# One decoder layer on one core: two loop steps swapped, two loads moved into the loop, and the cross attention's row in another order

## What is computed

```python
x = x + attn(layernorm(x))          # gated delta rule with spikes, 8 heads, 64 keys, 128 values
x = x + xattn(layernorm(x), ctx)    # 16 heads of 64, context of 77 tokens
x = x + sign_ffn(layernorm(x))      # 128 -> 512 -> 512 -> 128, weights +1 or -1
```

```python
mem = 0.9 * mem + sd;  hard = mem > 0.5;  mem = mem - 0.5 * spike
s = s * alpha[..., None]
s = s + beta * outer(k, v - k @ s)
out = s @ q
```

## Time and profile before

| | us |
|---|---|
| median of 3 runs | 1318.04 |
| lowest, highest | 1312.53, 1323.74 |
| the profiled execution | 1319.52 |
| its span | 1317.8 |
| PE busy in the span | 1088.8 |
| DVE, ACT, POOL busy | 723.7, 503.0, 203.8 |

### The profile page before, as it was taken

How to read it: one execution, slowest core, us unless ns; L and a number is a source line. 1 busy time by engine, 2 the same in 40 slices (tenths; PEclk the granted TensorE clock), 3 DMA queues, 4 the chain that set the end, 5 groups by cost and what they waited for, 6 DMA issues and landing times. The chain is left out here.

```text
span 1317.8 us, 40766 instructions
## 1 busy us (share of the span) xinstructions
PE 1088.8 (83%) x17172; PEld 792.1 (60%) x17172; DVE 723.7 (55%) x2523; ACT 503.0 (38%) x1445; POOL 203.8 (15%) x381
## 2 busy tenths in 40 slices
PE   1577357999999999999999995777889889898867
PEld 1222126888888888888888883455447445545642
DVE  5657787787788878788665531252226134323500
ACT  1564111244444444444444333243244234424411
POOL 4000210112222112222211201111002001100200
PEclk9688655799999999999998887896989899999969
DMA  2000000000000000000000004000000000000000
GB/s 80 0 1 1 0 0 1 4 4 4 4 4 4 4 3 4 4 4 4 4 4 4 3 3 132 8 0 1 0 8 8 2 9 0 8 0 1 9 0 8
DMA packets 11219, 11.35 MB, mean 9 GB/s; under 512 B 1515, under 2 KB 9311, under 8 KB 11039
## 3 DMA queue, kind: packets, MB, share of 16 engines
q1 hardware_dynamic: 11039, 8.75, 2.2%
HBM read 7.70 MB, written 1.05 MB: 7 GB/s over the span
## 5 line engine op out<-in xcount | busy, mean ns | idle before, releaser
L830 PE MATMUL banks<-work 64*64 64x64 f32 x3072 | 110.0, 236 | 9.6 <-DVE gates L712 6.3
L1006 ACT COPY work<-banks 128x128 f32<-128x128 f32 x160 | 42.9, 268 | 180.9 <-PE banks L860 180.9
L860 PE MATMUL banks<-work,gates 64*64 64x32 f32 x2560 | 109.7, 224 | 1.2 <-issue 1.1
L717 DVE TENSOR_TENSOR work<-work,banks 128x128 f32<-128x128 f32 x128 | 37.0, 289 | 131.5 <-PE banks L870 130.5
L298 DVE SCALAR_TENSOR_TENSOR gates<-mom,gates 128x16 f32<-128x16 f32 x512 | 100.5, 196 | 10.5 <-ACT gates L414 5.9
L880 PE MATMUL banks<-work 64*64 64x32 f32 x2560 | 106.2, 223 | 0.0
L870 PEld LDWEIGHTS banks<-work 64*64 64x64 f32 x2048 | 77.2, 141 | 46.9 <-ACT work L1006 23.5
L870 PE MATMUL banks<-work 64*64 64x32 f32 x2048 | 87.1, 226 | 19.6 <-DVE work L722 16.9
L860 PEld LDWEIGHTS banks<-work,gates 64*64 64x64 f32 x2560 | 95.5, 141 | 12.0 <-issue 11.4
L712 DVE COPY_PREDICATED gates<-work,banks 128x256 f32<-128x256 uint32 x192 | 101.3, 528 | 1.1
L302 DVE SCALAR_TENSOR_TENSOR mom<-gates 128x16 f32<-128x16 f32 x512 | 98.0, 191 | 5.9
(11 more groups left out here) (225 smaller groups left out, 2380.2 us busy)
## 6 DMA issues: line engine op xcount, KB each, us to landing
work<-in_x_dram SPq DMA_DIRECT2D x4, 256.0 KB, 4.3
out_dram<-work SPq DMA_DIRECT2D x4, 256.0 KB, 3.5
gates<-in_w_ff_dram SPq DMA_DIRECT2D x3, 256.0 KB, 4.6
wv_sb<-in_wv_dram SPq DMA_DIRECT2D x1, 512.0 KB, 4.7
work<-in_w_out_dram SPq DMA_DIRECT2D x1, 512.0 KB, 4.9
gates<-in_x_Wq_dram SPq DMA_DIRECT2D x1, 512.0 KB, 6.3
gates<-in_x_Wk_dram SPq DMA_DIRECT2D x1, 512.0 KB, 6.9
gates<-in_x_Wv_dram SPq DMA_DIRECT2D x1, 512.0 KB, 7.8
```

The lines of the kernel that those rows point to most:

```text
L830: last = pe.matmul(level_out(l)[to, a], KS[rows, n.two, hp], late[rows, hp], start=True, stop=True)
L860: last = pe.matmul(packed(psZX, l)[rows, hp], EA[rows, n.three, l, hp], first_half(X, l)[rows, hp], start=True, stop=True)
L1006: ac.copy(first_half(Z[:, l - 1], l), packed(psZX, l)).then_inc(z_ok, 1)
```

## The change

In the loop, add_xt and make_xt go ahead of the level steps. SP loads the context and w_out as soon as the last beta product is done (before, the region that they go to holds gate weights); VectorE scales w_out at the end of its body of round 30. In the tail:

- `front_u1` of rows 1 to 3 goes behind `project_out`; `front_out` is dealt out as (0), (1), (2, 3), (4, 5), (6), (7) instead of (0), (1, 2), (3, 4), (5), (6), (7). The context's transposes go behind `front_u1` of row 0.
- The first output of `connect_second` is made in pieces around `spread_root` and `feed_forward`; `keys` waits for it at its fifth product only.
- `context_values` goes ahead of `spread_root(b, 1)` and uses banks 2 and 7; `queries` uses banks 4 to 6; ScalarE keeps the values ahead of the queries; the scores no longer wait for the values, the first `weigh` does.
- ScalarE keeps a block's weighed sums behind the first kept quarter of the next block; of the last block VectorE keeps one half.

```diff
@@ loop, sync
+                sp.wait_ge(beta_mm, GATES)
+                sp.dma_start(ctx_sb, ctx_in.rearrange("b s d -> s b d")).then_inc(ctx_ld, 16)
+                sp.dma_start(wout_sb, w_out.rearrange("(h v) d -> v h d", v=DV)).then_inc(wout_ld, 16)
@@ loop, vector
+                def scale_out():
+                    ve.wait_ge(wout_ld, 16)
+                    for h in range(2 * HP):
+                        ve.tensor_scalar(wout_sb[:, h, :], wout_sb[:, h, :], v("w_hn", h), None, ALU.mult)\
+                            .then_inc(wout_ok, 1)
...
                         spike(scan, h + 1)
+                        if nxt:
+                            add_xt(nxt, l)
+                        spike(scan, h + 2)
                         if aft:
                             prefix(aft, l)
-                        spike(scan, h + 2)
+                        spike(scan, h + 3)
                         if aft:
                             suffix(aft, l)
-                        spike(scan, h + 3)
+                        spike(scan, h + 4)
                         if aft:
                             keep(aft, l)
-                        spike(scan, h + 4)
-                        if nxt:
-                            add_xt(nxt, l)
...
+                    if cur and cur.it == ROUNDS - 2:
+                        scale_out()
@@ loop, tensor
                             make_x(nxt, l)
+                        if nxt:
+                            make_xt(nxt, l)
                         if aft:
                             level(aft, l)
-                        if nxt:
-                            make_xt(nxt, l)
@@ tail, tensor
-                def connect_second(b, f, ps):
+                def connect_second(b, f, ps, parts):
                     pe.wait_ge(h1_ok, (b + 1) * F2)
                     if f >= 1:
                         pe.wait_ge(h2_ok, b * F2 + f)
-                    for a in range(F2):
+                    for a in parts:
...
-                        if a >= 4:
-                            pe.wait_ge(q2_ok, b * XP + a - 3)
-                        pe.matmul(bank[4 + a % 4][:, :], Wq_sb[:, a, :], n1, start=True, stop=True).then_inc(q2_mm, 1)
+                        if a >= 3:
+                            pe.wait_ge(q2_ok, b * XP + a - 2)
+                        pe.matmul(bank[4 + a % 3][:, :], Wq_sb[:, a, :], n1, start=True, stop=True).then_inc(q2_mm, 1)
...
                 def project_out(b):
-                    pe.wait_ge(xo_done, (b + 1) * 2 * NTB)
+                    pe.wait_ge(xo_done, (b + 1) * (2 * NTB - 1))
+                    pe.wait_ge(xo_late, b + 1)
...
                     if now:
-                        front_u1(b)
+                        if b == 0:
+                            front_u1(b)
+                            turn_context()
+                            pe.wait_ge(wout_ok, 2 * HP)
                         front_out(b, (0,))
                     if b:
                         project_out(done)
+                        if now:
+                            front_u1(b)
...
                     if b:
-                        connect_second(done, 0, bank[1])
+                        connect_second(done, 0, bank[1], (0, 1))
                     if now:
                         spread_root(b, 0)
+                    if b:
+                        connect_second(done, 0, bank[1], (2,))
+                    if now:
                         feed_forward(b)
+                    if b:
+                        connect_second(done, 0, bank[1], (3,))
+                    if now:
...
                         mean_square(b, 1)
+                        context_values(b)
                         spread_root(b, 1)
                         queries(b)
-                        context_values(b)
                         pe.wait_ge(kb_ok, b * 4 + 4)
-                        pe.wait_ge(vb_ok, b * 2 + 2)
@@ tail, scalar
                 def keep_weighed(b, n):
                     ac.wait_ge(weigh_mm, b * NTB + n + 1)
-                    for j in range(2):
+                    for j in range(2 if n + 1 < NTB else 1):
...
                         keep_centred(b, 1)
                         keep_keys(b)
-                        ac.copy(cb, ctxT[:, b]).then_inc(cb_ok, 1)
+                        keep_values(b)
                         for a in range(XP):
...
                             keep_turned(b, n, 0)
+                            if n:
+                                keep_weighed(b, n - 1)
                             keep_turned(b, n, 2)
...
-                        if now:
-                            keep_weighed(b, n)
+                    if now:
+                        keep_weighed(b, NTB - 1)
@@ tail, vector
+                def keep_weighed_late(b):
+                    ve.wait_ge(weigh_mm, (b + 1) * NTB)
+                    for a in range(4):
+                        last = ve.tensor_scalar(XO[:, 4 + a, (NTB - 1) * P:], bank[7][:, a * P:(a + 1) * P],
+                                                v("bv", 4 + a), None, ALU.add)
+                    last.then_inc(xo_late, 1)
...
                 for b in range(B + 1):
                     done, now = b - 1, b < B
+                    if b:
+                        add_attention(done)
                     if now:
                         front_act(b)
...
+                        keep_weighed_late(b)
```

More of the change, by code:

```diff
@@ L457, in _ @@
                             .then_inc(mconst, 1)
+        used[0] = 0
+        wout_sb = region([2 * HP, D])
+        ctx_sb = region([B, D])[0:S]
+        rows_start = used[0]
+        assert rows_start <= HP * P + HP * 2 * DK + HP * P
+        ctx_ld, wout_ld, wout_ok = sem("ctx_ld"), sem("wout_ld"), sem("wout_ok")
         used[0] = kept_end
@@ L597, in decoder_kernel, with _ @@
         with nc.Block() as block:
+            @block.sync
+            def _(sp):
+                sp.wait_ge(beta_mm, GATES)
+                sp.dma_start(ctx_sb, ctx_in.rearrange("b s d -> s b d")).then_inc(ctx_ld, 16)
+                sp.dma_start(wout_sb, w_out.rearrange("(h v) d -> v h d", v=DV)).then_inc(wout_ld, 16)
             @block.gpsimd
@@ L1261, in _, with turn_context @@
             def _(pe):
-                pe.wait_ge(ctx_ld, 16)
-                for j in range(B):
-                    last = pe.transpose(bank[0][:, j * S:(j + 1) * S], ctx_sb[:, j, :], ident[0:S, 0:S])
-                last.then_inc(ctx_mm, 1)
+                def turn_context():
+                    pe.wait_ge(ctx_ld, 16)
+                    for j in range(B):
+                        last = pe.transpose(bank[0][:, j * S:(j + 1) * S], ctx_sb[:, j, :], ident[0:S, 0:S])
+                    last.then_inc(ctx_mm, 1)
                 def centre(src):
@@ L1370, in context_values @@
                     for j in range(2):
[L1371 removed]
+                        last = pe.matmul((bank[2], bank[7])[j][0:S, :], cb, Wv_sb[:, j * 512:(j + 1) * 512],
                                          start=True, stop=True)
@@ L1400, in weigh @@
                     if i:
-                        pe.wait_ge(xo_done, 2 * i)
+                        pe.wait_ge(xo_done, 2 * i - b)
+                    if b and n == 0:
+                        pe.wait_ge(xo_late, b)
                     for h in range(XH):
@@ L1425, in _ @@
                     if now:
-                        front_out(b, (1, 2))
+                        front_out(b, (1,))
                     if b:
@@ L1431, in _ @@
                     if now:
-                        front_out(b, (3, 4))
+                        front_out(b, (2, 3))
                     if b:
@@ L1435, in _ @@
                     if now:
-                        front_out(b, (5,))
+                        front_out(b, (4, 5))
                     if b:
@@ L1472, in _ @@
                     if b:
-                        connect_second(done, 1, bank[3])
+                        whole(done, 1)
                     if now:
@@ L1476, in _ @@
                     if b:
-                        connect_second(done, 2, bank[3])
+                        whole(done, 2)
                     for n in range(NTB):
@@ L1485, in _ @@
                             if n == 0:
-                                connect_second(done, 3, bank[3])
+                                whole(done, 3)
                             if n == 1:
@@ L1495, in _ @@
             def _(ac):
-                ac.wait_ge(ctx_mm, 1)
-                ac.copy(ctxT, bank[0][:, 0:B * S].rearrange("p (b s) -> p b s", b=B)).then_inc(ctx_ok, 1)
                 def square(src, b, k):
@@ L1550, in keep_keys, with keep_values @@
                             last.then_inc(kb_ok, 1)
+                def keep_values(b):
+                    ac.wait_ge(vb_mm, b + 1)
+                    for j in range(2):
+                        ac.copy(VB[:, j * 512:(j + 1) * 512], (bank[2], bank[7])[j][0:S, :]).then_inc(vb_ok, 1)
                 def exponent(b, n):
@@ L1583, in _ @@
                         front_sig(b)
```

(11 more changed lines are left out.)

36 lines of the change are left out of this document (13 added, 23 removed).

## The result

The changed kernel takes 1249.4 us (median of 4 runs, 1247.3 to 1257.0) against 1317.7 us before (4 runs, 1312.5 to 1323.7) on the same chip: ratio 0.948, 95% interval 0.943 to 0.954. That is 68.4 us less where 46.3 were forecast, and outside the range on the fast side. The profiled execution took 1257.0 us (span 1255.3), granted clock 0.909 in the mean against 0.892. A ratio leaves out slow runs, those over 1.5% above the fastest of their kernel, so it can differ a little from the quotient of two medians, and of the profiled executions a_piece's alone is a slow one.

The account below looks back on a forecast made before the run. TensorE was taken to bound the loop, and a chain of waits with no engine full the tail. Loop 14.4, loads 6.2 and tail 25.7 sum to 46.3 us off the median 1318.0: 1271 us forecast, range 1255 to 1291.

Parts of the forecast that it names:

- Part 1: Loop, XT product ahead of the level product: 14.4 us less, 13.0 in 20 scan rounds and 1.4 in 11 after.
- Rival B: Loop gives nothing because VectorE passes the 0.43 us delay on: 1285 us, 18%.
- D: Loop: the chain of level products is a round's true bound, so the kernel gets slower: 1353 us, 4%.
- Part 2: Loads between loop and tail: u1 starts 7.0 us earlier, less 0.8 for the context's transposes, net 6.2 us.
- Part 3: Tail without the loads: reordered steps fill or shorten TensorE's waits, 25.7 us less, bounds 12 and 32.
- (c): Tail rows 1 to 3: first sign layer in pieces placed in two TensorE gaps, 1.6 us a row.
- (e): Tail, turned weights: copy ahead of the activations, transposes run early; net 1.25 us a row, 4.5 in row 0.
- (d): Tail: context_values moved into spread_root's wait for GpSimd's power, net 1.6 us a row.
- (a): Tail, weighed sums: four of eight last activations to VectorE, u1 into the gap before centre; net 1.0 us a row.
- (b): Tail rows 1 to 3: front_out 4 and 5 together ahead of centre(x2) shrink a 0.8 us gap, 0.75 us gained.
- Rival C: Tail gives half because steps meet the next wait: 1284 us, 12%.
- rival A: Tail: TensorE's clock stays up at the queries and partly in the weighing, 10 us more, 1261 us, 22%.

Follow-up runs that it names:

- a_piece: Changed kernel with the first sign layer (first output of connect_second) made at once again, ahead of spread_root: 1255.1 us, ratio 0.953 to the kernel before.
- b_tail: Kernel before with only the tail's reordering, loop order and loads as before: 1277.5 us, ratio 0.965.
- b_load: Kernel before with only the early loads and scaling of w_out and the context's transposes behind the first u1: 1317.5 us, ratio 0.995.
- f_end: Changed kernel with unread idle products in the waits of the pass behind row 3: 1242.0 us, ratio 0.941 to the kernel before.
- b_fill: Kernel before with two unread idle products per row in the gap between mean_square and spread_root: 1310.8 us, ratio 0.992.
- f_u1: Changed kernel with u1 ahead of the out projection again: 1246.4 us, ratio 0.946 to the kernel before.
- f_same: Changed kernel once more with nothing altered, as reference: 1253.0 us, ratio 0.947 to the kernel before.
- g_after: Changed kernel with unread idle products ahead of the loop's first round: 1246.0 us, ratio 0.944 to the kernel before.

## Why the prediction was wrong by a third, point by point

**Part 1.** Scan rounds: 13.0 us forecast, 13.3 measured in the mean over all traces (10.8 in the pair of before and after alone): right, although the wait for the masked copy was five times what I had put. Rounds behind the scan: 0.13 forecast, 0.54 measured, 4.9 us over nine rounds where I had 1.4 for eleven: the step that took 0.26 us at L870 and gave 0.13 back counted one level's wait; the runs don't say which of the others shrank too. The terms add up to 18 us, and the runs give 17 to 26: part 1 is worth more than 14.4, about 18 to 20. Rival B (the loop gives nothing) and D (the level chain bounds it) are out.

**Part 2.** The 7.0 of the gap and the 0.8 of the transposes are right to 0.1 us by the trace. What failed is the cover for the ten loads behind them: TensorE waits 2.6 us longer for GpSimd's first power. From last power to span's end the changed kernel takes 470.1 us and b_tail 472.1, so on the new tail part 2 gives 2.0 us, not 6.2. On the old tail, by b_load, it gives 6 to 7, though the same wait is there; that the clock makes the difference is not shown.

**Part 3.** The waits were priced about right: 27.7 us of idle time against 25.7 in the whole tail, and by the single edits (c) 1.3 us a row against 1.6, (e) 1.7 against 1.25, the moved work of (d) 1.2 against 1.6, u1's gap 1.07 against 0.83. The halved copy of the weighed sums in (a) and the front products of (b) have no run of their own. Rival C is out. The rows gained 10.7 us each and not 6.2, and the single edits say why: (d) carries 2.2 us and (e) 1.5 us a row beyond their waits. Against the 507 us that the old tail took in all but the profiled execution of before, part 3 alone is 45.5 us shorter, where 25.7 were forecast.

**The step that failed** is the paragraph on the clock. It saw the fall to 0.50 at the queries, named the gap behind which it comes, priced it at 2.9 us a row at most, and then put the whole of it in rival A at 22% and nothing in the sum. The queries alone gave 7.7 us (36.2 us in four rows before, 28.6 after). The argument against A, that small products and transposes stay, did not hold: in the changed kernel they stay and the clock is 1.00 at the queries. What A still underpriced is the rest of the rows, the weighing above all: 17.8 us by the busy time of the same instructions, where A had 10. The missing 22 us, by the runs: the clock in the tail +18, the waits of part 3 +2, part 2 -4, the loop +4 to +6.

Edit (a) at the end after row 3, 1.0 us, came: the last out projection waits 1.32 us for its copies where it waited 2.27. It stands in the table under rows 1 to 3, since the end is counted from the start of this product. The 61.0 us of the end have the clock below its upper level before and after (0.71 in the mean from 1194 to 1204 us), and the out projection takes 9.86 us for the same 16 passes that take 7.29 in f_end.

The Trainium skill (TensorE: Matmul & The Clock Gate, Part 1) calls the throttled state the default, which activity releases. The pairs with idle products agree: 9.13 and 9.88 us without, 7.13 with. The start of the loop agrees only in part: the clock rose there with idle products, and fell again in rounds in which TensorE shows 22.9 of 25 us busy.

## What to carry to other kernels

Where a chain of steps leaves gaps on TensorE and wide fp32 products behind them take longer than the same products elsewhere in the trace, put the difference into the sum: filling the gap is worth its work and the clock too (here 1.2 and 2.2 us a row). Before moving real work for it, try a product that nobody reads, one line in the gap. It shows whether there is clock to win, and it can be a cure itself (14 us here, on top of the change). It does not give the whole price: on the kernel before it won 4 us of the tail, and part 3 has 18 by the clock. It paid where TensorE bounded what followed; ahead of a stretch that VectorE bounds it gave nothing. And compare the busy time of the same instructions before and after: what it loses is not a wait.

Where a load is moved ahead, look at what stood behind it: here the sign weights stayed where they were, and the work that needs them became the next wait (2.6 us).

## What the runs showed of the hardware that I had not expected

- The granted clock fell to its lower level behind waits of only 0.8 to 2.3 us between groups of small products, and the steps behind took up to 1.9 times as long: 32 weighed products 3.68 us against 1.97, eight wide passes 6.57 against 3.67.
- It also falls in the loop's rounds of 64x64 products, where TensorE is hardly idle: 0.50 between 740 and 750 us in the kernel before, behind 10 us with 8.30 busy. The same code in b_fill was busy for 8.45 us of those 10 and stayed at 1.00, so the busy time doesn't say which. A loop of such products thus has a part of its time that no edit explains: the two rounds behind 221 us took 40.2 us in f_u1's profiled execution and 49.5 in f_same's, some 9 of the 7 to 19 us by which the runs that the ratios use differ within one kernel.
- The tail, a chain of one wait after the other, scatters less: 465.8, 465.7 and 465.8 us in three executions of one code (after, f_same, g_after) in which u1 starts at 789.6, 786.2 and 778.4 us. But it has jumps of 2 to 4 us where the code is the same: the old row 0 takes 104.0 us in one execution and 107.0 to 107.8 in three others, the end behind row 3 61.0 us in f_same and 57.9 in f_u1.
